# Bias pieces of a pair of heads moved behind its four long score matmuls, the two row halves in turns

## What is computed

```
q, k, v = (layernorm(x) @ Wqkv + bqkv), 16 heads of 16
scores = q @ k.T / 4 - slope[head] * |i - j|
out = softmax(scores) @ v, then @ Wout + bout; x = x + out
```

## Time and profile before

| | |
|---|---|
| median of three runs | 3318.08 us (3310.41 to 3332.55) |
| profiled execution, span from first to last instruction | 3314.4 us |
| its mean granted TensorE clock | 0.961 |
| TensorE matmul busy | 3139.1 us, 95% |
| TensorE weight loads busy | 1960.7 us, 59% |
| VectorE busy | 2521.7 us, 76% |
| ScalarE busy | 1985.8 us, 60% |

### The profile page before, as it was taken

One profiled execution on the slowest core, in us unless ns is written; L12 is line 12 of the kernel. 1 busy time (PEld: TensorE's weight loads), 2 busy tenths in 40 slices (PEclk: granted clock), 3 DMA queues, 4 the chain that ended last, 5 costly groups with the idle time before them and its releaser, 6 DMA issues. The chain is left out here.

```text
span 3314.4 us, 79004 instructions
## 1 busy us (share of the span) xinstructions
PE 3139.1 (95%) x31780; PEld 1960.7 (59%) x31780; DVE 2521.7 (76%) x4848; ACT 1985.8 (60%) x2967; POOL 780.8 (24%) x916
## 2 busy tenths in 40 slices
PE   7999999995999689999999999999999999998999
PEld 3666666663888555555555555555555555546888
DVE  6777777755888478778878788788787887837887
ACT  2544555432666317776767676767676766775665
POOL 3445454532222201111110110111111101002222
PEclk8999999986999759999999999999999999998999
DMA  1000000003111422122222131222221312202111
GB/s 54 15 15 27 27 28 27 21 15 105 52 52 51 100 39 46 25 49 47 46 50 46 25 71 25 46 50 46 50 43 27 66 30 42 42 12 95 52 58 39
DMA packets 110349, 145.51 MB, mean 44 GB/s; under 512 B 21792, under 2 KB 94256, under 8 KB 109200
## 3 DMA queue, kind: packets, MB, share of 16 engines
q1 hardware_dynamic: 108776, 136.78, 17.5%
q0 software_dynamic: 768, 2.77, 0.4%
q10 hardware_dynamic: 440, 0.90, 0.2%
HBM read 53.79 MB, written 38.24 MB: 28 GB/s over the span
## 5 line engine op out<-in xcount | busy, mean ns | idle before, releaser
L1896 DVE TENSOR_REDUCE b_half_max<-banks 128x1 f32<-128x512 f32 x2048 | 1304.3, 685 | 290.5 <-PE banks L1560 174.9
L1814 ACT ACTIVATE b_p_t<-banks 128x1024 f32<-128x1024 f32 x1024 | 1040.3, 1026 | 372.1 <-PE banks L1560 231.2
L1639 PE MATMUL banks<-b_k_stack,b_q_stack 62*128 62x512 f32 x2048 | 835.0, 480 | 26.4 <-issue 10.4
L1701 PE MATMUL banks<-b_q_stack,b_k_stack 64*128 64x512 f32 x2048 | 832.9, 469 | 8.8 <-ACT b_p_t L1814 7.7
L1655 PE MATMUL banks<-b_p_t,b_v 128*17 128x256 f32 x8192 | 628.4, 385 | 0.2 <-ACT b_p_t L1814 0.2
L1701 PEld LDWEIGHTS banks<-b_q_stack,b_k_stack 64*128 64x128 f32 x2048 | 344.4, 185 | 373.0 <-issue 322.8
L1639 PEld LDWEIGHTS banks<-b_k_stack,b_q_stack 62*128 62x128 f32 x2048 | 342.0, 188 | 75.5 <-DVE b_half_max L1896 33.9
L1560 PE MATMUL banks<-b_unit,b_tables 64*128 64x64 bf16 x4096 | 373.1, 197 | 0.0
L1137 ACT ACTIVATE ffn_relu<-banks,ffn_scale_fc 128x512 f32<-128x512 f32 x256 | 176.2, 688 | 205.3 <-PE banks L1069 205.3
L1082 PE MATMUL banks<-ffn_proj_t,ffn_r_hi 128*128 128x256 f32 x1024 | 262.2, 289 | 2.7 <-DVE ffn_r_lo L1263 2.5
L1560 PEld LDWEIGHTS banks<-b_unit,b_tables 64*128 64x128 bf16 x4096 | 186.2, 96 | 120.7 <-issue 70.6
(11 more groups left out here) (247 smaller groups left out, 4937.7 us busy)
## 6 DMA issues: line engine op xcount, KB each, us to landing
ffn_x<-x SPq DMA_DIRECT2D x32, 512.0 KB, 3.8
b_q_stack<-b_qk_hi SPq DMA_DIRECT2D x252, 64.0 KB
b_k_stack<-b_qk_hi SPq DMA_DIRECT2D x252, 64.0 KB
a_x<-hidden_states SPq DMA_DIRECT2D x16, 512.0 KB, 4.1
x<-a_x SPq DMA_DIRECT2D x16, 512.0 KB, 2.9
x<-ffn_x SPq DMA_DIRECT2D x16, 512.0 KB, 2.8
b_x<-x SPq DMA_DIRECT2D x8, 1024.0 KB, 5.5
out<-ffn_x SPq DMA_DIRECT2D x16, 512.0 KB, 2.9
```

Source lines behind the costliest of these rows:

```text
L1639: last = pe.matmul(m, q_stack[rows, slot, qb * P:(qb + 1) * P], k_stack[rows, slot, half * BANK:(half + 1) * BANK], start=True, stop=not h ...
L1701: last = pe.matmul(out, k_stack[stack, slot, kb * P:(kb + 1) * P], q_stack[stack, slot, half * BANK:(half + 1) * BANK], start=True, stop=n ...
L1814: act.activation(p_t[use % P_BUFS][:, :, :], scores[use % 2], ACT.Exp, scale=slopes()[pair][0]).then_inc(p_made, 1)
L1896: dve.tensor_reduce(half_max[:, (pair + rg * PAIRS) * QB + qb, half:half + 1], misc.at["max", g, turn], axis=AX.X, op=ALU.max, negate=True ...
```

## The change

The loop of `attend` takes a pair of heads in one step in place of two. On TensorE it issues column long, row long, column long, row long, in the same order of row halves as before; then the pieces of both column scores, then those of both row scores. `add_block_bias` takes a list of row halves and issues the first piece of each, then the second of each. Each last piece counts up its semaphore, as before. `find_maxima` issues the pieces of two row scores behind the second one. On the other engines a step stands for two as well, and the waits on all semaphores keep their values. `side_by_side` is called with half as many steps for the loop, so other work is placed between whole pairs.

```diff
@@ schedule
             def lead():
-                for _ in range(STEPS + LEAD):
-                    for _ in range(row_parts):
+                for _ in range((STEPS + LEAD) // ROWGROUPS):
+                    for _ in range(ROWGROUPS * row_parts):
                         next(rows)
                     yield
...
-                side_by_side(*([(STEPS, attend(g, rows), 1)] if g >= 0 else []),
-                             *([(STEPS + LEAD, lead(), 1)] if g == -1 else []),
+                side_by_side(*([(STEPS // ROWGROUPS, attend(g, rows), 1)] if g >= 0 else []),
+                             *([((STEPS + LEAD) // ROWGROUPS, lead(), 1)] if g == -1 else []),
@@ tensor
-            def add_block_bias(out, g, pair, rg, variant):
-
-                rows = slice(rg * STACK, (rg + 1) * STACK)
+            def add_block_bias(outs, g, pair, variant, ready):
+
                 for part in range(PARTS):
                     cols = slice(part * STACK, (part + 1) * STACK)
-                    last = pe.matmul(out[:, cols], tables[rows, g % GROUPS * PAIRS + pair, 1 - variant, part, :], unit[rows, :],
-                                     start=False, stop=part == PARTS - 1, tile_position=(rg * STACK, 0))
-                return last
+                    for rg, out in outs:
+                        rows = slice(rg * STACK, (rg + 1) * STACK)
+                        last = pe.matmul(out[:, cols], tables[rows, g % GROUPS * PAIRS + pair, 1 - variant, part, :], unit[rows, :],
+                                         start=False, stop=part == PARTS - 1, tile_position=(rg * STACK, 0))
+                        if part == PARTS - 1:
+                            last.then_inc(ready, 1)
@@ find_maxima
-                        if not here:
+                        if here:
+                            outs.append((rg, m[:, at:at + P]))
+                        else:
                             last.then_inc(row_scores, 1)
+                    yield
+                    if turn % ROWGROUPS == ROWGROUPS - 1:
+                        if outs:
+                            add_block_bias(outs, g, pair, int(qb >= CT), row_scores)
+                            outs = []
                         yield
-                        if here:
-                            add_block_bias(m[:, at:at + P], g, pair, rg, int(qb >= CT)).then_inc(row_scores, 1)
                         yield
@@ attend on TensorE
-                for t, half, kb, pair, rg in turns(g):
-                    first, slot = place(g, pair + rg * PAIRS)
-                    stack, use = slice(first, first + STACK), 2 * t + pair
-                    out, here, at = scores[use % 2][:, rg, :], kb // CT == half, kb % CT * P
+                for t, half, kb, pair in pair_turns(g):
+                    here, at = kb // CT == half, kb % CT * P
+                    use, outs = PAIRS * t + pair, []
                     if use >= 2:
                         pe.wait_ge(p_made, use - 1)
-                    last = pe.matmul(out, k_stack[stack, slot, kb * P:(kb + 1) * P], q_stack[stack, slot, half * BANK:(half + 1) * BANK],
-                                     start=True, stop=not here, tile_position=(first, 0))
-                    if not here:
-                        last.then_inc(col_scores, 1)
+                    for rg in range(ROWGROUPS):
+                        first, slot = place(g, pair + rg * PAIRS)
+                        stack, out = slice(first, first + STACK), scores[use % 2][:, rg, :]
+                        last = pe.matmul(out, k_stack[stack, slot, kb * P:(kb + 1) * P], q_stack[stack, slot, half * BANK:(half + 1) * BANK],
+                                         start=True, stop=not here, tile_position=(first, 0))
+                        if here:
+                            outs.append((rg, out[:, at:at + P]))
+                        else:
+                            last.then_inc(col_scores, 1)
+                        next(rows, None)
+                    if here:
+                        add_block_bias(outs, g, pair, int(kb < CT), col_scores)
                     next(rows, None)
-                    if here:
-                        add_block_bias(out[:, at:at + P], g, pair, rg, int(kb < CT)).then_inc(col_scores, 1)
                     next(rows, None)
-                    if rg == ROWGROUPS - 1:
-                        follow(t, pair)
+                    follow(t, pair)
                     yield
...
```

More of the change, by code:

```diff
@@ L1483, in row_turns, with pair_turns @@
                 yield g, turn, pair, qb, half, 1 - turn % 2
-        def turns(g):
+        def pair_turns(g):
             for half in range(HALVES):
@@ L1489, in turns @@
                     for pair in range(PAIRS):
-                        for rg in range(ROWGROUPS):
-                            yield (g * HALVES + half) * QB + kb, half, kb, pair, rg
+                        yield (g * HALVES + half) * QB + kb, half, kb, pair
         def tails(weigh, conclude):
@@ L1805, in attend @@
             def attend(g, rows):
-                for t, half, kb, pair, rg in turns(g):
-                    if rg == ROWGROUPS - 1:
-                        use = 2 * t + pair
-                        act.wait_ge(col_scores, ROWGROUPS * (use + 1))
-                        if use >= P_BUFS:
-                            act.wait_ge(weighed, 2 * (t - 2))
-                        if use == 0:
-                            act.wait_ge(weights_split, 3)
-                        act.activation(p_t[use % P_BUFS][:, :, :], scores[use % 2], ACT.Exp, scale=slopes()[pair][0]).then_inc(p_made, 1)
-                    next(rows, None)
-                    if rg == ROWGROUPS - 1:
-                        follow(t, pair)
+                for t, half, kb, pair in pair_turns(g):
+                    use = PAIRS * t + pair
+                    act.wait_ge(col_scores, ROWGROUPS * (use + 1))
+                    if use >= P_BUFS:
+                        act.wait_ge(weighed, 2 * (t - 2))
+                    if use == 0:
+                        act.wait_ge(weights_split, 3)
+                    act.activation(p_t[use % P_BUFS][:, :, :], scores[use % 2], ACT.Exp, scale=slopes()[pair][0]).then_inc(p_made, 1)
+                    for rg in range(ROWGROUPS):
+                        next(rows, None)
+                    follow(t, pair)
                     yield
@@ L1932, in attend @@
             def attend(g, rows):
-                for t, half, kb, pair, rg in turns(g):
-                    next(rows, None)
-                    if rg == ROWGROUPS - 1:
-                        follow(t, pair)
+                for t, half, kb, pair in pair_turns(g):
+                    for _ in range(ROWGROUPS):
+                        next(rows, None)
+                    follow(t, pair)
                     yield
```

## The result

| | before | changed |
|---|---|---|
| median, alternating runs, 20 each | 3316.18 us (3310.41 to 3336.07) | 3331.80 us (3320.59 to 3347.79) |
| ratio with its 95% interval | | 1.0038 (1.0024 to 1.0051) |
| profiled execution, span | 3314.4 us | 3328.9 us |
| its mean granted TensorE clock | 0.961 | 0.954 |
| first to last unit of the attention loop | 1734.5 us | 1745.1 us |

Forecast was 3286 us with a range of 3260 to 3318, so the time lies outside it, on the slower side. Of the 14.5 us between the spans 10.6 lie inside the loop of units and 3.2 ahead of it.

A forecast was written before the change was run, and what follows sets the result against it. TensorE was taken to bound the attention stage, VectorE not far behind. A gain of 1.00 us a group over 30.75 groups made 31 us off 3318, 3287; 1 to 2 us more gave 3286 us, range 3260 to 3318.

The forecast's parts named there:

- the one on VectorE: Row-score reductions in the loop: scores released late make the next unit's row score wait, 0.25 us lost a group of 32 units.
- The clock is no term of the sum: Attention stage: TensorE's granted clock is full (2.4 GHz) in nearly every slice, so it was given no share in the sum.
- The group without other work: A group of 32 units: 1.28 + 0.15 - 0.25 - 0.18 = 1.00 us gained, over 30.75 groups 31 us.
- lost at three places a group: Off the column diagonal: late release delays the next unit's second row score by 0.08 us, three of five places unhidden.
- third to fifth unit together: First half of the q and k projection goes behind the third unit: 0.15 us saved a group in place of 0.23.
- hide it: Units with column pieces behind a late release: their pieces end later than the delayed long, so the 0.08 us is hidden.
- the turn, three units: Turn of a group, where row maxima hang on all reductions: net loss of 0.18 us for two units, their gains included.
- The first term, 55 us: Pieces moved behind the longs: 0.075 us less on average for 738 units, 55 us if nothing but TensorE mattered.
- The third, VectorE takes more: Rival: VectorE or ScalarE takes more, VectorE standing still after each unit with row pieces; 3303 us, chance 0.25.
- The full gain: Rival: VectorE absorbs the late release in pauses that other tiles' work gives it; 3318 - 55 = 3263 us, chance 0.15.
- the gain that isn't there: Rival: pieces and longs hinder each other anywhere, or the second load isn't made ahead; 3318 us, chance 0.05.
- The slower rival: Rival: piece loads behind the longs are no longer hidden, a round costs up to 0.095 us; 3370 us, chance 0.1.

The follow-up runs named there:

- runs 9 and 10: Statistics of the later seven batches over 32 of 256 columns, in the kernel before (9: 3315.18 us) and in the changed kernel (10: 3306.00 us).
- run 4: The changed kernel with both pieces of one row half ahead of both of the other, not in turns: 3328.93 us, ratio 1.0032 to the kernel before.
- run 8: The changed kernel with row pieces ahead of column pieces and the projections one unit earlier: 3314.76 us, ratio 0.9984 to the kernel before.
- run 2: The kernel before with steps of whole pairs but the old places of the pieces: 3315.74 us, ratio 0.9983 to the kernel before.
- run 5: The changed kernel with the row scores' pieces ahead of the column scores' pieces: 3316.49 us, ratio 0.9993 to the kernel before.
- runs 6 and 7: Row-maxima reductions over 256 columns in place of 512, in the kernel before (6: 3286.04 us) and in the changed kernel (7: 3258.59 us).
- run 3: The changed kernel with the first projection one unit earlier (weight 4 in place of 3): 3317.49 us, ratio 1.0000 to the kernel before.
- run 1: The changed kernel's order of pieces, with other work placed by half units as in the kernel before: 3332.66 us, ratio 1.0045 to the kernel before.
- 11: The changed kernel with row pieces first and the statistics in two blocks of four, three units apart: 3305.48 us, ratio 0.9949 to the kernel before.

## Why the prediction was wrong

**The step that failed** is the one on VectorE, with the sum built on it. It asked where a late release meets a VectorE without slack, and looked for the answer in stretches of reductions alone. It said of batches with other work that they "give VectorE more room". One piece of other work is VectorE's own: the statistics, 3.3 us in one go, in every fourth group. There the late release and the shorter units add 0.55 and 0.32 of waiting, and with the clock behind them 2.5 to 3.8 us a group, 21.7 in all; with short statistics (runs 9 and 10) the change gains 9 us. The row was there: the wait of 0.77 at 1957.45 in the trace of before, in a list that I did not go through by the work beside it.

**"The clock is no term of the sum"** failed with it, and was the larger part: by the group of run 4 with the same waits and a full clock, some 15 of the 21.7 us. With the 6 us of the waits alone the loop would have come out some 5 us ahead of before, 15 less than 10.6. The step was read from the level that the earlier trace rows shows, full, but a change that lengthens a wait can move the clock. The length of the wait does not settle it, though: with 1.33 and 0.32 it fell in six of seven equal groups (run 4), with 0.76 in three of seven (run 8), with the 0.77 of before and the 0.95 of run 2 in none. What decides between equal groups no run here shows, so how often it falls is in part luck of the execution.

**The group without other work** gained 0.5 and not 1.0. Its units by their median over the quiet groups, before and changed, in the names of the prediction:

| | before | changed | forecast |
|---|---|---|---|
| row or column pieces, bound by TensorE | 1.375 | 1.30 | 1.30 |
| eight pieces | 1.45 | 1.36 | 1.38 |
| no pieces, or column pieces, behind a unit with row pieces | 1.22, 1.37 | 1.28, 1.37 | lost at three places a group; "hide it" |
| third to fifth unit together | 7.00 | 6.90 | 0.15 less |
| behind the short unit at the change of the half | 2.70 | 2.95 | 0 |
| the turn, three units | 5.63 | 5.71 | 0.18 lost in two, 0.07 gained in one |

- The unit lengths are right, and so is their mechanism: +0.34, a load at +0.11, bursts of 0.31. Here the trace speaks a second time against the rule of the Trainium skill (page TensorE: Matmul & The Clock Gate, Part 3) that a load overlaps matmuls only of another row group: the load at 2036.49 runs beside a matmul of its own row half, and the change's 0.08 a unit come from just that.
- "Where the next unit has column pieces, they hide it" was wrong: in the program the column pieces stand behind the second row long, so what delays that long delays them. Four units a group lose their 0.07. Row pieces first (run 5) gave it back: 1.30.
- The unit behind the short one lost 0.25. In the changed kernel's timeline its row-score load at 2049.50 waits 0.48 for a reduction. With the reductions at half length it loses 0.24 too (2.44 to 2.68, runs 6 and 7). I had given 0 to the short units and not looked at the one behind them.
- The third to fifth unit (0.10 for 0.15) and the turn (0.08 lost, forecast 0.18 - 0.07 = 0.11) are sizes.

**The first term, 55 us,** can't be had as it stands, since VectorE costs even the old order some 30; between the short-reduction twins, the order is worth 27.5 us, 35 in the loop. Of the other 20 some 11 are in the seven normalizing groups: there the twins differ by 0.25 and not by the 1.8 that 55 us over 30.75 groups make, with that wait of 0.60. The 0.24 of the unit behind the short one would be another 6, if it is the same in the other 24 groups.

**The rivals.** The third, VectorE takes more, was the right direction with the wrong place: it priced it at every unit and came to 3303. The full gain fell with the result, and the gain that isn't there with 7 against 6, where the order is worth 27.5 us. The slower rival had the sign for another reason: eight pieces take 0.31, some 0.04 a round beyond the first, and never 0.095. No case held the time, and the 0.1 for slower stood for a mechanism that did not happen. For a rival on the slower side I should have asked for the longest thing that VectorE does between two reductions.

What stays open: why the clock falls in one group and not in an equal one; what takes back the rest of the gains of 3 and 5 together; and the 6 against 15 us of wait and clock in other executions, since it rests on one profiled execution of each kernel.

## What to carry to other kernels

Moving small work behind large work also moves the release of the results, and the engine that consumes them pays where it has least slack: list the longest foreign block on each near-bound engine (here 3.3 us of statistics among reductions of 0.61) and redo the sum there, not in the stretch that is easiest to read. Release first what the engine nearest its limit waits for (row pieces first: 15 us), and lay that engine's own long blocks beside foreign work of the bound engine (19 us even without the change). Look at the granted clock behind each longer wait, in slices of a few us and over several equal groups: here 0.9 us of added waiting cost up to 3.8. Twins that shorten the suspect in the old and the new order show what a change is worth without it; one kernel alone would have credited the order of the pieces with all of the 26 to 28 us.

## What the runs showed of the hardware

- The granted clock of TensorE fell to 0.50 (1.2 of 2.4 GHz) with no wait longer than 1.33 us ahead of it at the statistics, for 3.4 or 6.8 us each time. Of the seven normalizing groups of a trace it fell in all with a wait of 1.32 us (changed kernel), in six with 1.33 (run 4), 1.31 (run 5) and 1.20 (run 1), in two with 0.86 (run 3), in three with 0.76 (run 8), and in none with 0.77 (before) and 0.95 (run 2). So equal waits go with either level, and a shorter one did not keep it full.
- Between equal groups of one kernel, 3.4 us at half clock cost 1.4 to 1.5 us (runs 1, 3, 4, 5 and 11) and 6.8 us cost 2.5 to 2.9 (runs 1, 3, 4 and 8).
- Bf16 pieces of the two row halves overlap alike, whether they are issued in turns or one half after the other (3331.8 and 3328.9 us).
- Eight pieces in one burst take 0.31 us, four 0.23: each further round costs 0.04, the rate that the earlier trace rows shows.
